# A two-layer cross network on one core: the sums and the weighing of TensorE become one loop of 16 unit pairs, with ScalarE copying slots to a fixed place

## The reference

```python
# x: (512, 39, 64)   W0: (39, 39, 128)   W1: (39, 128, 128)
def _cin_forward(x, Ws):
    x0 = x
    h = x
    outs = []
    for W in Ws:
        h = jnp.einsum('bid,bjd,ijh->bhd', x0, h, W)
        outs.append(h)
    out = jnp.concatenate(outs, axis=1)
    return out.sum(axis=-1)          # (512, 256)
```

## Time and profile before

| | us |
|---|---|
| median of 3 runs | 345.33 |
| lowest and highest of them | 340.78, 349.36 |
| the profiled execution's own time | 343.26 |
| its span, first to last instruction | 341.5 |
| mean granted TensorE clock of the profiled execution | 0.93 |

### The profile page before, as it was taken

One profiled execution on the slowest core, in us unless ns is written; L12 is line 12 of the kernel. 1 busy time (PEld: TensorE's weight loads), 2 busy tenths in 40 slices (PEclk: granted clock), 3 DMA queues, 4 the chain that ended last, 5 costly groups with the idle time before them and its releaser, 6 DMA issues.

```text
span 341.5 us, 16183 instructions
## 1 busy us (share of the span) xinstructions
PE 263.6 (77%) x7325; PEld 226.8 (66%) x7325; DVE 200.4 (59%) x671; ACT 129.1 (38%) x270; POOL 114.8 (34%) x284
## 2 busy tenths in 40 slices
PE   0999999206946516848988788899798878889997
PEld 0555555106935515738878778788788778779996
DVE  1125599999436977935567675686577766730000
ACT  1477777203954415511333234323343224322000
POOL 9425596304022694662233222332232222300000
PEclk9999999755996968876999999999999999999999
DMA  7800000400034625622334443353335433200000
GB/s 263 370 0 0 5 0 0 161 1 0 2 111 136 184 68 189 195 56 101 101 101 145 114 142 118 105 192 103 102 112 168 131 105 103 73 23 19 0 2 15
DMA packets 10860, 32.56 MB, mean 95 GB/s; under 512 B 1200, under 2 KB 1712, under 8 KB 10672
## 3 DMA queue, kind: packets, MB, share of 16 engines
q1 hardware_dynamic: 10224, 31.15, 28.4%
q10 hardware_dynamic: 576, 0.52, 0.4%
HBM read 31.14 MB, written 0.52 MB: 93 GB/s over the span
## 4 chain that ended last, share of the span: by engine, by line
PE 70%; issue 17%; DVE 5%; ACT 4%; DMA 2%; POOL 2%; SPq 0%; DVEq 0%; POOLq 0%
PE out_ps L611 31%; PE stage L591 22%; PE stage L568 16%; DVE arena L425 3%; ACT arena L517 3%; DVE arena L422 2%; DMA arena<-in_w 2%; PE stage L576 2%; POOL arena L286 1%; ACT arena L542 0%; ACT arena L531 0%; POOL arena L290 0%; SPq L298 0%; SPq L297 0%; ACT arena L524 0%
## 5 line engine op out<-in xcount | busy, mean ns | idle before, releaser
L591 PE MATMUL stage<-arena 64*32 64x115 f32 (+4 forms) x6144 | 87.0, 244 | 45.2 <-issue 32.6
L611 PE MATMUL out_ps<-arena 128*128 128x128 f32 x920 | 111.3, 280 | 4.4 <-issue 4.4
L542 ACT COPY arena<-stage 128x460 f32<-128x460 f32 x128 | 63.1, 545 | 132.9 <-PE stage L591 131.4
L611 PEld LDWEIGHTS out_ps<-arena 128*128 128x128 f32 x920 | 106.5, 194 | 9.1 <-issue 8.6
L591 PEld LDWEIGHTS stage<-arena 64*32 64x32 f32 x6144 | 75.5, 110 | 53.7 <-issue 51.0
L286 POOL TENSOR_TENSOR arena<-arena 128x24 f32<-128x24 f32 x96 | 52.8, 575 | 158.7 <-PE stage L591 144.1
L422 DVE TENSOR_TENSOR arena<-arena 128x224 f32<-128x224 f32 (+1 forms) x192 | 62.1, 389 | 71.2 <-PE stage L591 71.1
L425 DVE TENSOR_TENSOR arena<-arena 128x392 f32<-128x392 f32 (+5 forms) x288 | 91.4, 386 | 0.0
L568 PE MATMUL stage<-arena 128*128 128x390 f32 x156 | 54.3, 511 | 7.7 <-DMA arena<-in_w 7.7
L338 DVE TENSOR_TENSOR arena<-arena 128x294 f32<-128x294 f32 (+30 forms) x189 | 47.5, 327 | 15.1 <-ACT arena L513 15.0
L568 PEld LDWEIGHTS stage<-arena 128*128 128x128 f32 x156 | 30.8, 198 | 30.5 <-issue 10.4
(11 more groups left out here) (7 smaller groups left out, 2.2 us busy)
## 6 DMA issues: line engine op xcount, KB each, us to landing
arena<-in_x_d SPq DMA_DIRECT2D x32, 448.0 KB, 4.0
arena<-in_x_w SPq DMA_DIRECT2D x32, 360.0 KB, 3.3
arena<-in_w SPq DMA_DIRECT2D x1, 1344.0 KB, 10.1
arena<-in_c SPq DMA_DIRECT2D x2, 640.0 KB, 11.7
arena<-in_w SPq DMA_DIRECT2D x2, 390.0 KB, 3.4
arena<-in_w SPq DMA_DIRECT2D x1, 768.0 KB, 7.4
out<-arena ACTq DMA_DIRECT2D x4, 128.0 KB, 1.7
arena<-in_w SPq DMA_DIRECT2D x1, 384.0 KB, 5.9
```

The costliest lines, as they stand in the source:

```text
L542: nc.scalar.copy(view(s0[n % 2] + s * PAIRS + t, (B, LISTED), (1, FOUR)), banks[2 * (q % 2) + s][:, 0:LISTED * FOUR].rearrange("p (n b) -> ...
L591: done = nc.tensor.matmul(banks[2 * four_place + s][WIDE * column:WIDE * (column + 1), 0:LISTED * FOUR] .rearrange("p (n b) -> p b n", b=F ...
L611: done = nc.tensor.matmul(to, view(s0[n % 2] + k * B, (1, B)), weights, start=k == 0, stop=k == LISTED - 1, skip_group_check=True)
```

## The change

- **One loop on TensorE.** Batch 0 stays a loop of 4 passes over two units. Units 8 to 31 become a loop over batches 1 to 3, each with an inner loop of 4 passes over two units; both loops together make 16 unit pairs. A unit now has its sums, then 13 calls of weighing in two halves of 6 and 7 (`weigh_staged`). The address in `c0` is computed from the loop's register. The 11 slots that are left (10 singles and the last paired) are weighed at the end of a batch (`weigh_rest`). The weighing of the last batch is still written out in full at the end. Waits of TensorE go by registers that are counted up.
- **Fixed place.** In each unit of batches 1 to 3 ScalarE copies the 13 slots that the unit weighs from `s0` to `t_0`, in halves of 768 and 896 words a partition, and signals `staged`; TensorE signals `weighed` for each half, and a half's place is overwritten only when it has been weighed. At the end of a batch the 11 remaining slots go the same way.
- **One `out_ps` bank** instead of two. TensorE opens it by a product with zeros over its 256 columns (`begin_out`), once a batch, and waits for ScalarE's `take_out` before that (`out_free`). GpSimd zeroes the identity for it.
- **Small products.** In batch 0 VectorE makes the 5 small products (20 instructions a unit); GpSimd makes them from unit 8 on, and TensorE waits for `rest_ready` from there only.
- **Loads.** `DS` goes from 3 to 2. A load of `x_d` for unit u goes out when unit u-2 has been used up.
- **ScalarE's start.** The first two `singles` stand ahead of the copies of the turns, not behind.
- `dynamic_dma_scratch_size` goes from 4096 to 1024, and the arena from 56064 to 56832 words.

```diff
-    PRODS, WS, DS = 2, 2, 3
+    PRODS, WS, DS = 2, 2, 2
+    IN_BATCH = PAIRS // UNIT
+    EACH = PAIRED // IN_BATCH
+    HALVES = [(0, EACH // 2), (EACH // 2, EACH)]
+    REST = LISTED - IN_BATCH * EACH
...
+            pool.wait_ge(filled, SETUP_BANKS)
+            nc.gpsimd.memset(ident, 0.0).then_inc(out_free, 1)
-            for u in range(UNITS):
+            for u in range(IN_BATCH, UNITS):
                 pool.wait_ge(d_loaded[u % DS], 16 * (u // DS + 1))
...
             def load_listed(u):
                 if u >= DS:
                     sp.wait_ge(prod_ready, u - DS + 1)
-                    sp.wait_ge(rest_ready, u - DS + 1)
+                    if u - DS >= IN_BATCH:
+                        sp.wait_ge(rest_ready, u - DS - IN_BATCH + 1)
                     sp.wait_ge(singles_ready, u - DS + 1)
...
-            for u in range(WS, UNITS):
-                if u + 1 < UNITS and u + 1 >= DS:
-                    load_listed(u + 1)
+            for u in range(DS, UNITS):
+                load_listed(u)
                 load_windows(u)
...
+                    if n % 2 == 0 and u < IN_BATCH:
+                        mult(view(at + n * n // 2, T, (1, n // 2)), view(x_at, D, (1, n // 2)),
+                             view(x_at + n // 2, D, (1, n // 2)), ALU.mult)
+                for column, slot, w, b0, b1 in LONE_LISTS if u < IN_BATCH else ():
+                    mult(view(to + column * LISTED + slot, T, (1, b1 - b0)), view(d + D_B + b0, D, (1, b1 - b0)),
+                         view(d + D_LONE, D, (0, b1 - b0)), ALU.mult)
...
             def take_out(n):
-                act.wait_ge(batch_done, n + 1)
+                act.wait_ge(weighed, IN_ALL * (n + 1) if n < BATCHES - 1 else IN_ALL * n + 1)
...
+            def stage(first, a, b, half):
+                if half >= 2:
+                    act.wait_ge(weighed, half - 1)
+                nc.scalar.copy(view(t_0 + a * B, (1, (b - a) * B)), view(first + a * B, (1, (b - a) * B)))\
+                    .then_inc(staged, 1)
...
+                if n >= 1 and t % UNIT == 0:
+                    for i, (a, b) in enumerate(HALVES):
+                        half = (n - 1) * IN_ALL + v * len(HALVES) + i
+                        stage(s0[(n - 1) % 2] + (SINGLES + v * EACH) * B, a, b, half)
...
+            def begin_out():
+                nothing = view(ident0, (1, HID))
+                nc.tensor.matmul(out_ps[:, 0:2 * HID], nothing, view(ident0, (0, 2), (1, HID)), start=True, stop=False,
+                                 skip_group_check=True)
+            def weigh_staged(v, a, b):
+                for k in range(a, b):
+                    done = weigh(t_0 + k * B, c0 + k * HID + v * (EACH * HID), False)
+                done.then_inc(weighed, 1)
...
+            def turn(w_wanted, unit_wanted, banks_wanted, ahead, behind):
+                for v in range(PRODS):
+                    ahead()
+                    pe.wait_ge(w_loaded[v], w_wanted)
+                    pe.wait_ge(prod_ready, unit_wanted)
+                    pe.wait_ge(singles_ready, unit_wanted)
+                    pe.reg_add(unit_wanted, unit_wanted, 1)
+                    for half in range(2):
+                        pe.wait_ge(emptied, banks_wanted)
+                        pe.reg_add(banks_wanted, banks_wanted, 2)
+                        sum_four(v, half, half)
+                    behind(v)
+                pe.reg_add(w_wanted, w_wanted, 16)
...
                 with pe.Fori(0, IN_BATCH // PRODS):
+                    turn(w_wanted, unit_wanted, banks_wanted, lambda: None, lambda v: None)
+                pe.wait_ge(c1_ready, 1)
...
+                with pe.Fori(1, BATCHES):
+                    pe.wait_ge(out_free, out_wanted)
+                    pe.reg_add(out_wanted, out_wanted, 1)
+                    begin_out()
+                    with pe.Fori(0, IN_BATCH, PRODS) as first:
+                        def weigh_unit(v):
+                            for a, b in HALVES:
+                                staged_half()
+                                weigh_staged(first + v, a, b)
+                        turn(w_wanted, unit_wanted, banks_wanted, rest_in, weigh_unit)
+                    for a, b in REST_HALVES:
+                        staged_half()
+                        weigh_rest(t_0, t_0 + SINGLES * B, a, b).then_inc(weighed, 1)
+            s_at = s0[(BATCHES - 1) % 2]
+            pe.wait_ge(out_free, BATCHES)
+            begin_out()
+            pe.wait_ge(emptied, emptied_through_four(FOURS - 1))
+            for k in range(IN_BATCH * EACH):
+                weigh(s_at + (SINGLES + k) * B, c0 + k * HID, False)
+            weigh_rest(s_at, s_at + (LISTED - 1) * B, 0, REST).then_inc(weighed, 1)
```

More of the change, by code:

```diff
@@ L142, in cin_kernel @@
         d_0 = take(DS * UNIT * D_WORDS)
+        t_0 = take(EACH * B)
         out_sb0 = take(2 * HID)
@@ L155, in cin_kernel @@
         c1_second0 = d_0 + Y_WIDTH
-        assert w0_second0 + Y_WIDTH <= d_0 and c1_second0 + SINGLES * HID <= out_sb0
+        assert REST <= EACH and w0_second0 + Y_WIDTH <= d_0 and c1_second0 + SINGLES * HID <= out_sb0
         banks = [ctx.enter_context(nc.psum_tensor(f"stage{i}", [P, BANK], F32)) for i in range(6)]
-        out_ps = [ctx.enter_context(nc.psum_tensor(f"out_ps{i}", [P, BANK], F32)) for i in range(2)]
+        out_ps = ctx.enter_context(nc.psum_tensor("out_ps", [P, BANK], F32))
         RING = len(banks)
@@ L179, in cin_kernel @@
         singles_ready = sem("singles_ready")
[L180 to L181 removed]
+        staged = sem("staged")
+        weighed = sem("weighed")
+        out_free = sem("out_free")
         out_stored = sem("out_stored")
@@ L508, in _, with singles @@
         def _(act):
+            def singles(u):
+                act.wait_ge(d_loaded[u % DS], 16 * (u // DS + 1))
+                nc.scalar.copy(view(prod0 + u % PRODS * UNIT * PROD, (PROD, UNIT), (LISTED, 4), (1, SINGLES)),
+                               view(d_0 + u % DS * UNIT * D_WORDS + D_SINGLES, (D_WORDS, UNIT), (SINGLES, 4), (1, SINGLES)))\
+                    .then_inc(singles_ready, 1)
             g = 0
@@ L514, in _ @@
                     g += 1
+            act.wait_ge(z_ready, 1)
+            for u in range(PRODS):
+                singles(u)
             for k, n in TURNS:
@@ L549, in _ @@
                 if t == PAIRS - FOUR and n >= 1:
+                    (a, b), (_, c) = REST_HALVES
+                    half, s_at = n * IN_ALL - len(REST_HALVES), s0[(n - 1) % 2]
+                    stage(s_at, a, b, half)
+                    act.wait_ge(weighed, half)
+                    nc.scalar.copy(view(t_0 + b * B, (1, (SINGLES - b) * B)), view(s_at + b * B, (1, (SINGLES - b) * B)))
+                    nc.scalar.copy(view(t_0 + SINGLES * B, (1, (c - SINGLES) * B)),
+                                   view(s_at + (SINGLES + IN_BATCH * EACH) * B, (1, (c - SINGLES) * B)))\
+                        .then_inc(staged, 1)
                     take_out(n - 1)
@@ L597, in sum_four @@
                 done.then_inc(filled, 1)
[L599 to L614, removed]
@@ L622, in _ @@
                 pe.reg_mov(banks_wanted, emptied_through_four(-2))
+                pe.reg_mov(staged_wanted, 1)
+                pe.reg_mov(out_wanted, 1)
+                pe.reg_mov(rest_wanted, 1)
                 with pe.Fori(0, IN_BATCH // PRODS):
[L624 to L646, removed]
@@ L647, in _, with staged_half, rest_in @@
-            for k in range(LISTED):
-                weigh(BATCHES - 1, k)
+                    turn(w_wanted, unit_wanted, banks_wanted, lambda: None, lambda v: None)
+                pe.wait_ge(c1_ready, 1)
+                def staged_half():
+                    pe.wait_ge(staged, staged_wanted)
+                    pe.reg_add(staged_wanted, staged_wanted, 1)
+                def rest_in():
+                    pe.wait_ge(rest_ready, rest_wanted)
+                    pe.reg_add(rest_wanted, rest_wanted, 1)
```

41 lines of the change are left out of this document (22 added, 19 removed).

## The result

The changed kernel takes 315.69 us (median of 4 runs, 315.39 to 316.88) against 346.70 for the kernel before in the same comparison (340.78 to 349.36): a ratio of 0.921, interval 0.910 to 0.932. The profiled execution took 315.39 us with a span of 313.6, 1.8 us of it around the span as before. The forecast was 327: the direction and the wide range (313 to 345) held, the forecast's own range (322 to 332) did not. Between the two profiled executions, from which the forecast was worked out, the gain is 343.26 - 315.39 = 27.9 us where 16.2 had been worked out.

What follows compares the result with a forecast made beforehand. TensorE was taken to wait for written-out code drawn from memory, about 0.93 us a unit. Gains of 14.9 us from unit 10 on and 1.3 before it, 16.2 off 343.26, gave 327; own range 322 to 332, wide range 313 to 345.

Steps and rivals of the forecast that it cites:

- Units 10 to 31: From unit 10's start to TensorE's end: instruction stalls go, 177.3 us becomes 162.4, a gain of 14.9 us.
- the back edges: Loop turns of TensorE between unit pairs: 11 at 0.20 us, 2.2 us in all, bounds 0 to 4.3.
- a unit's work: TensorE's sums and 26 weighing records without stalls: 5.61 us a unit, 123.5 us for 22 units.
- The batch end: Eleven weighing calls, ScalarE's copy with signals, and `begin_out`: 3.6 us, three times 10.8 us.
- The register addresses: Weighing calls' addresses from a register: cost 0, at most 0.2 us a call; rival that they are dear, chance 0.20.
- Staging: ScalarE's copies to the fixed place: cost 0, with ScalarE busy 4.7 to 5.3 of 5.61 us a unit.
- another pace: Rival: ScalarE or the loads set the pace at 6.3 us a unit, adding 15 us: 342; chance 0.07.
- The hold at unit 8: GpSimd, arriving at 128.9, is held until VectorE pauses at 139.7; TensorE waits 7.6 us, until 141.2.
- GpSimd not held: Rival at unit 8: VectorE pauses for a load, GpSimd slips in, unit 10 starts 9.4 us earlier: 318; chance 0.23.
- Units 8 and 9 behind the hold: At low clock, unit 8 takes 11.6 us and unit 9 7.6; unit 10 starts at 160.4, before 161.68.
- Unit 7's sums: End of batch 0: TensorE follows VectorE by 2.5 us and has unit 7 summed at 133.6, before at 139.3.
- the early singles: Start of batch 0: two copies no longer stand between the last turn and the first sums, worth 0.7 us.

Runs made afterwards that it cites:

- e1: Changed kernel with TensorE's program for units 8 to 31 written out again, staging, halves and one bank kept: 344.52 us, 0.998 of the kernel before.
- e3: Changed kernel with the loop's weights taken from fixed addresses, without the register computation ahead of each weighing call: 315.79 us.
- e10: Changed kernel with every staged half copied twice by ScalarE: 319.24 us.
- e5: Changed kernel with the small products of all 32 units on VectorE and GpSimd's loop left out: 310.69 us, 0.903 of the kernel before.
- e2: Changed kernel with the small products of units 8 and 9 on VectorE too, GpSimd making them from unit 10 on: 311.18 us.
- e9: Changed kernel with ScalarE's first two copies of singles behind the copies of the turns again: 315.71 us.
- e12: e1 with each of a unit's 13 weighing calls 170 columns wide instead of 128: 357.34 us.
- e4: Changed kernel with all small products of all units on GpSimd, as in the kernel before: 317.07 us.

## Why the prediction was right, and where its sizes were off

*What bounds the kernel.* Right. The idle time named "issue" was code being drawn; e1 brings it back by undoing the loop alone, with 39 packets. The forecast fell short of the gain by 11.7 us: 4.9 from unit 10 on (14.9 worked out, 19.8 measured) and 6.7 ahead of it (1.3 and 8.0), to a tenth.

*Units 10 to 31.* The mechanism is right; the term was mis-sized. Predicted from the start of unit 10 to TensorE's end: 162.4 us. Measured: 311.1 - 153.6 = 157.5. Of the 4.9 us, 2.2 are the back edges, taken at 0.20 us and measured at 0, and 2.7 a unit's work, 5.49 us instead of 5.61. The price of a unit was taken from TensorE's busy time, and part of the stalls' price was in there: in the kernel before, too, sums without a stall took 2.39 us and 28 weighing records 3.32 (0.1186 each), but sums broken by a stall took 2.6 (1.86 + 0.76 at unit 10). The batch end was right: 3.6 against 3.67. The register addresses were rightly taken at 0 (e3).

*Staging.* Rightly taken at 0, with a wrong load: 4.7 to 5.3 us of 5.61 leaves little room, e10 points to 3.8 of 5.49. The rival "another pace" had its weight from that error.

*The hold at unit 8.* Right, and it was the doubtful step. GpSimd was held in VectorE's run until its pause and TensorE started unit 8 at 139.6, against 141.2. The rival (GpSimd not held) gives 318 us, nearer to what was measured than the forecast, but that is luck: the hold was there.

*Units 8 and 9 behind the hold.* This is the step that failed. They were priced by unit 9 of the kernel before, 6.9 us for sums and 5.09 for weighing, 19.2 us together. Measured from 139.62 to 153.62, where the timeline has unit 10 start (the chain's pieces end 0.07 later): 14.0. The changed kernel's chain there:

```profile
139.62 3.58 PE stage L634 x120
143.19 1.32 PE out_ps L650 x7
144.52 2.38 PE out_ps L650 x19
146.90 1.30 PE stage L634 x66
148.20 1.10 issue
149.30 1.28 PE stage L634 x48
150.59 3.10 PE out_ps L650 x26
```

The row that was used had a stall of 3 us for code in the middle of its sums, at the low clock. In the changed kernel no such stall lies in unit 8, and the clock came back within its weighing (1.32 us for 7 records, then 2.38 for 19). The sum counted the drawing of code for a unit that had waited 5.55 us, time in which code could be drawn: in e5 and e2, without that wait, the stalls of units 8 and 9 are 2.8 and 2.4 us, in the changed kernel 1.1. e1, with the wait and the same two units written out, has 0.3; so it was not the loop that took the stall of 3 us away. Unit 8 took 7.2 us instead of 11.6, unit 9 6.8 instead of 7.6.

*Batch 0.* The small terms hold: VectorE's unit is 4.88 us (109.96 to 114.84), worked out as 4.87. Unit 7's sums ended at 133.2, predicted 133.6, but by two errors that nearly cancel: its products were there 1.6 us earlier, and its sums took 3.38 us instead of 2.5, as at the low clock. The first pass and the set-up were 1 to 2 us quicker than taken over from the kernel before. The 0.7 us for the early singles was wrong (e9): a term was counted whose cover, TensorE's own delay of a microsecond, was not looked for.

*The sum of the miss.* 327 - 315.4 = 11.6 us, to a tenth: 4.9 in units 10 to 31, 5.2 in units 8 and 9, 1.6 in the start of unit 8.

*What stays open.* Why written-out code costs 1.2 us a unit in e1 and 0.93 in the kernel before. The trace of e1 has 25.1 us of idle time from unit 10 on against 20.5, and its clock falls behind some stalls, while that of the kernel before stays at 1.00 there; but why the stalls are longer, and why those of the kernel before, of up to 1.9 us, leave the clock alone, no run tells. How the 7.7 us in units 8 and 9 divide between the hold, the stall and the clock of the kernel before. And where between 1000 and 1850 instructions a loop ceases to stay.

## What to carry to other kernels

Idle time of TensorE called "issue" that comes back every unit or two, with a packet of the instruction queue for every 250 instructions or so beside it, was here a price of written-out code; a loop whose pass holds under a thousand of TensorE's instructions took it away at once, even if another engine must copy data to a fixed place for it. Count the pass: at twice that length the loop was worse than straight code. When work is moved off an engine that is held by another, look at the moment at which the rest of it will next start, and at who needs its result by then: here the hold moved by three units. Taking that engine out removed it, and letting it join two units later left a hold of 5.78 us that TensorE, by then with more work than VectorE in each unit, did not have to wait for.

## What the runs showed of the hardware

- A loop of 900 to 1000 TensorE instructions drew one packet in 131 us; one of about 1850 drew 45 in 176 us, with waits of up to 3.6 us, and took 376 us in all against 345 for straight code.
- Time added to TensorE's matmuls was mostly added to the stalls of straight code, not hidden in them: 19.6 us in the loop, 12.8 in straight code (16 by the ratios), with 7 us less of idle time in the trace.
- After some stalls for code the granted clock fell: in e12 a weighing took 5.62 us at 0.70 behind a stall of 1.83 us, where it took 3.95 at 1.00.
- GpSimd instructions that read what is in SBUF, coming into an unbroken run of VectorE instructions with two operands, were held 9.6 us (changed kernel), 9.9 and 9.7 us (e4), 10.5 and 9.6 us (kernel before), 5.8 us (e2), until VectorE paused, and not for one instruction. In e4 ten instructions of GpSimd that began together with a run of VectorE were through in 3.8 us, though that run went on for 9.5; what lets them through is not shown. Released together with VectorE, the same three took 1.13 us.
- ScalarE's copies start before the one ahead has ended: four of 0.545 us back to back in 1.87.
